# Macaron block with routed experts: FFN tiles in a deeper pipeline, three indirect DMAs under way, and a memset of a scratch between each and the next

## What is computed

```python
x = x + 0.5 * ffn(layernorm(x))
x = x + attn(layernorm(x))
x = x + 0.5 * ffn(layernorm(x))

def ffn(x):                       # xf: (8192, 128)
    top1 = argmax(xf @ gate_w.T + gate_b)
    for e in range(8):
        h = relu(xf @ w1[e].T + b1[e])
        y = h @ w2[e].T + b2[e]
        out = out + where(top1 == e, y, 0)
```

## Time and profile before

| | |
|---|---|
| Median of 3 runs | 652.54 us (649.6 to 659.46) |
| Profiled execution | 652.16 us, span 650.3 us |
| TensorE busy | 487.5 us |
| VectorE busy | 330.1 us |
| ScalarE busy | 263.2 us |
| GpSimd busy | 266.8 us, of which 264.3 us indirect DMAs |
| Mean granted TensorE clock | 0.874 |

### The profile page before, as it was taken

How to read it: one execution, slowest core, us unless ns; L and a number is a source line. 1 busy time by engine, 2 the same in 40 slices (tenths; PEclk the granted TensorE clock), 3 DMA queues, 4 the chain that set the end, 5 groups by cost and what they waited for, 6 DMA issues and landing times.

```text
span 650.3 us, 13261 instructions
## 1 busy us (share of the span) xinstructions
PE 487.5 (75%) x3914; PEld 434.7 (67%) x3914; DVE 330.1 (51%) x1229; ACT 263.2 (40%) x862; POOL 266.8 (41%) x288
## 2 busy tenths in 40 slices
PE   3983323989997999937788738487599798398986
PEld 2972313878886988926666526356499788388885
DVE  2553451545553655525799548464175554144442
ACT  1310001443443444526797547342245434144442
POOL 1156275555554444410000631615442555545543
PEclk9999997999997999965798658555699989789999
DMA  9923311556656655263000100331254564465640
GB/s 244 350 45 133 111 54 66 195 188 210 229 181 201 222 206 209 90 181 90 2 3 2 44 26 7 134 105 35 94 191 178 177 209 180 155 219 177 218 168 18
DMA packets 73189, 90.21 MB, mean 139 GB/s; under 512 B 11517, under 2 KB 49666, under 8 KB 72992
## 3 DMA queue, kind: packets, MB, share of 16 engines
q1 hardware_dynamic: 63760, 71.24, 32.8%
q0 software_dynamic: 8640, 17.52, 8.4%
q10 hardware_dynamic: 720, 0.60, 0.4%
HBM read 23.82 MB, written 19.62 MB: 67 GB/s over the span
## 4 chain that ended last, share of the span: by engine, by line
PE 54%; another core or an unknown queue 12%; DVE 10%; issue 9%; ACT 7%; DMA 4%; SPq 1%; POOL 0%; ACTq 0%; POOLq 0%; DVEq 0%
PE bank L1044 19%; PE classes L1057 16%; PE classes L1044 4%; ACT hT L483 3%; PE classes L1000 3%; PE bank L1032 2%; PE bank L990 2%; PE bank L1087 2%; DVE row_max L868 2%; DVE probs L870 2%; DMA x<-y_rows,tile_rows 2%; PE bank L1122 1%; PE classes L1108 1%; ACT k_by_head L522 1%
## 5 line engine op out<-in xcount | busy, mean ns | idle before, releaser
L439 POOL DMA_INDIRECT sorted_rows<-x_sb,rows x128 | 123.5, 965 | 221.8 <-DVE rows L701 166.8
L483 ACT ACTIVATE hT<-bank,stage_w 128x128 f32<-128x128 f32 x426 | 125.7, 366 | 195.3 <-PE bank L1044 156.1
L1044 PE MATMUL bank<-xT,stage_w 128*128 128x128 f32 x852 | 135.4, 298 | 36.6 <-ACT xT L475 28.9
L1057 PE MATMUL classes<-w_sb,hT 128*128 x1136 | 157.7, 284 | 0.1
L1044 PEld LDWEIGHTS bank<-xT,stage_w 128*128 128x128 f32 x852 | 112.6, 201 | 58.4 <-issue 58.2
L1057 PEld LDWEIGHTS classes<-w_sb,hT 128*128 128x128 f32 x1136 | 145.4, 200 | 0.6 <-issue 0.5
L447 POOL DMA_INDIRECT out_x<-y_rows,tile_rows x71 | 70.4, 991 | 78.6 <-DVE y_rows L799 42.0
L447 POOL DMA_INDIRECT x<-y_rows,tile_rows x71 | 70.4, 991 | 78.4 <-DMA x<-y_rows,tile_rows 28.2
L782 DVE TENSOR_SCALAR hT<-classes,stage_w 128x128 f32<-128x128 f32 x142 | 49.6, 349 | 101.6 <-PE classes L1044 64.0
L799 DVE SCALAR_TENSOR_TENSOR y_rows<-classes,residual 128x128 f32<-128x128 f32 x142 | 41.4, 291 | 73.2 <-PE classes L1057 49.0
L773 DVE TENSOR_SCALAR x_stage<-tile_rows 128x128 f32<-128x128 f32 x142 | 50.6, 358 | 23.2 <-DMA tile_rows<-sorted_rows 22.7
(11 more groups left out here) (114 smaller groups left out, 516.6 us busy)
## 6 DMA issues: line engine op xcount, KB each, us to landing
stage_w<-w_pack SPq DMA_DIRECT2D x142, 322.0 KB
tile_rows<-sorted_rows SPq DMA_DIRECT2D x142, 68.0 KB
x_sb<-x SPq DMA_DIRECT2D x16, 268.0 KB, 5.3
x_sb<-in_x SPq DMA_DIRECT2D x16, 256.0 KB, 5.5
w_pack<-in_w SPq DMA_DIRECT2D x1, 2048.0 KB, 9.5
w_sb<-in_w SPq DMA_DIRECT2D x1, 2048.0 KB, 10.6
sorted_rows<-x_sb,rows POOLq DMA_INDIRECT x128
sorted_rows<-filler SPq DMA_DIRECT2D x17, 68.0 KB
```

The costliest lines, as they stand in the source:

```text
L439: pool.indirect_dma_start(out=sorted_rows, out_offset=bass.IndirectOffsetOnAxis(ap=rows[k][:, t:t + 1], axis=0), in_=x_sb[:, groups[k][0] ...
L483: last = nc.scalar.activation(hT[:, n % 2, c, :], bank[n % 2][:, c * P:(c + 1) * P], ACT.Relu, bias=bias)
L1044: last = nc.tensor.matmul(mine, stage_w[:, w, c * P:(c + 1) * P], xT[:, n % 2, :], start=True, stop=True)
L1057: last = nc.tensor.matmul(bank[4 + n % 2][:, 0:D], hT[:, n % 2, c, :], w2_sb[:, bass.ds(expert, 1), c, :], start=(c == 0), stop=(c == HC - 1))
```

## The change

- Between two indirect DMAs GpSimd sets a scratch of 128x256 float32 to zero. A memset waits only for the memset before it.
- Three indirect DMAs are under way instead of two (`UNDER_WAY`).
- `pool_order`: the last group's 16 scatters are no longer paired with outputs. In the first FFN they come before all outputs, in the second after 14 outputs.
- SyncE: for the second and third span the rows of the first two quads are loaded before the weights of the first.
- The FFN tiles: four buffers for `x_stage` and `xT`, three for `hT`, `residual` and the hidden result's bank; TensorE's order becomes hidden(i), transpose(i + 2), output(i - 2). VectorE copies the transposed tile instead of ScalarE, ScalarE takes all four relus. VectorE normalizes four tiles ahead.
- `rank` of the last group comes after tile 12; ScalarE's and VectorE's waits for the expert weights before the first FFN are gone, as the weights' own slots are waited for.

```diff
+    AHEAD = 2
+    DEEP = 4
+    HIDDEN = 3
+    UNDER_WAY = 3
...
-        ahead = (0, 12)[f]
-        pool_order += early + outs[:ahead]
-        for row, tile in zip(final, outs[ahead:ahead + len(final)]):
-            pool_order += [row, tile]
-        pool_order += outs[ahead + len(final):]
+        ahead = (0, 14)[f]
+        pool_order += early + outs[:ahead] + final + outs[ahead:]
...
+    PAUSE = 256
...
-    RANK_TILE = 14
+    RANK_TILE = 12
...
                     sp.wait_ge(tabled, list_no[f, g] + 1)
-                    stage_weights(f, *quads[0])
+                    if g == 1:
+                        stage_weights(f, *quads[0])
                     wait_landed(sp, pool_no["rows", (f, g), groups[f, g][1] * R - 1])
...
-                        if q >= 2:
+                        if q >= 2 or g > 1:
                             stage_weights(f, *quads[q - 1])
...
             for q, item in enumerate(pool_order):
+                if q:
+                    if q >= 2:
+                        pool.wait_ge(paused, q - 1)
+                    nc.gpsimd.memset(pause[:], 0.0).then_inc(paused, 1)
...
-                    if q >= 2:
-                        pool.wait_ge(landed[q % 2], 16 * (q // 2))
+                    if q >= UNDER_WAY:
+                        pool.wait_ge(landed[q % UNDER_WAY], 16 * (q // UNDER_WAY))
...
-                    pool.wait_ge(y_ready, number(f, i) + 1)
-                    pool.wait_ge(landed[q % 2], 16 * (q // 2))
+                    pool.wait_ge(y_ready if f == 0 else y_summed, number(f, i) + 1)
+                    pool.wait_ge(landed[q % UNDER_WAY], 16 * (q // UNDER_WAY))
...
-                copy_xT(0)
                 for i in range(WORK):
                     relu(i)
-                    if i + 1 < WORK:
-                        copy_xT(i + 1)
...
-                stage(0)
-                stage(1)
-                for i in range(WORK):
-                    relu(i)
-                    if i + 2 < WORK:
-                        stage(i + 2)
-                    if i >= 1:
-                        take_output(i - 1)
-                    if i >= 2:
-                        dve.wait_ge(y_summed if f == 0 else y_ready, number(f, i - 1))
-                    add_residual(i)
-                    if f == 0 and i >= 1:
-                        take_moments(i - 1)
+                for i in range(DEEP):
+                    stage(i)
+                for i in range(AHEAD):
+                    copy_xT(i)
+                for i in range(WORK + AHEAD):
+                    if i + AHEAD < WORK:
+                        copy_xT(i + AHEAD)
+                    if i + DEEP < WORK:
+                        stage(i + DEEP)
+                    if i < WORK:
+                        add_residual(i)
+                    if i >= AHEAD:
+                        take_output(i - AHEAD)
+                    if f == 0 and i >= AHEAD + 1:
+                        take_moments(i - AHEAD - 1)
...
+                for i in range(AHEAD):
+                    transpose_x(i)
                 for i in range(WORK):
                     hidden(i)
-                    if i + 1 < WORK:
-                        transpose_x(i + 1)
-                    if i >= 1:
-                        output(i - 1, of_quad[(i - 1) % QUAD])
+                    if i + AHEAD < WORK:
+                        transpose_x(i + AHEAD)
+                    if i >= AHEAD:
+                        output(i - AHEAD)
```

More of the change, by code:

```diff
@@ L273, in macaron_kernel @@
         inv_sum = sb("inv_sum", [P, R * CLASS_HEADS])
+        pause = sb("pause", [P, PAUSE])
         attended = sb("attended", [P, 2, R * CLASS_HEADS, HEAD_DIM])
@@ L292, in macaron_kernel @@
         routed, tabled = sem("routed"), sem("tabled")
-        landed = [sem(f"landed{s}") for s in range(2)]
+        landed = [sem(f"landed{s}") for s in range(UNDER_WAY)]
         pads_stored = sem("pads_stored")
+        paused = sem("paused")
         rows_loaded = [sem(f"rows_loaded{q}") for q in range(QUADS)]
@@ L318, in ranks_of @@
             if k[1] == LAST:
-                return bank[7][:, 0:n]
+                return bank[3][:, 0:n]
             return bank[4][:, 256:256 + n]
         def wait_landed(eng, q):
-            for m in (q - 1, q):
-                if m >= 0:
-                    eng.wait_ge(landed[m % 2], 16 * (m // 2 + 1))
+            for m in range(max(q - UNDER_WAY + 1, 0), q + 1):
+                eng.wait_ge(landed[m % UNDER_WAY], 16 * (m // UNDER_WAY + 1))
         def load4(eng, which, table, i, top):
@@ L935, in _ @@
             whole(list_tiles((0, 3)))
-            dve.wait_ge(pack_loaded, 48)
             experts(0, {})
@@ L1039, in hidden @@
                     pe.wait_ge(xT_copied, n + 1)
+                    if n >= HIDDEN:
+                        pe.wait_ge(relu_done, n + 1 - HIDDEN)
                     for c in range(HC):
-                        mine = bank[n % 2][:, c * P:(c + 1) * P]
-                        if c >= HC_ACT:
-                            mine = bank[2 + n % 2][:, (c - HC_ACT) * P:(c - HC_ACT + 1) * P]
-                        last = nc.tensor.matmul(mine, stage_w[:, w, c * P:(c + 1) * P], xT[:, n % 2, :], start=True,
+                        last = nc.tensor.matmul(bank[n % HIDDEN][:, c * P:(c + 1) * P],
+                                                stage_w[:, w, c * P:(c + 1) * P], xT[:, n % DEEP, :], start=True,
@@ L1045, in hidden, with output @@
                                                 stop=True)
-                        if c == HC_ACT - 1:
-                            last.then_inc(h_a_done, 1)
-                    last.then_inc(h_v_done, 1)
-                def output(i, expert):
+                    last.then_inc(h_done, 1)
+                def output(i):
                     n = number(f, i)
                     if n >= 2:
-                        pe.wait_ge(y_ready, n - 1)
+                        pe.wait_ge(y_summed, n - 1)
+                    pe.wait_ge(relu_done, n + 1)
@@ L1054, in output @@
                     for c in range(HC):
-                        if c in (0, HC_ACT):
-                            pe.wait_ge(relu_a if c == 0 else relu_v, n + 1)
-                        last = nc.tensor.matmul(bank[4 + n % 2][:, 0:D], hT[:, n % 2, c, :],
-                                                w2_sb[:, bass.ds(expert, 1), c, :], start=(c == 0), stop=(c == HC - 1))
+                        last = nc.tensor.matmul(bank[4 + n % 2][:, 0:D], hT[:, n % HIDDEN, c, :],
+                                                w2_sb[:, bass.ds(expert[i], 1), c, :], start=(c == 0), stop=(c == HC - 1))
@@ L1059, in output, with load_experts @@
                     last.then_inc(y_done, 1)
                 listed = {spans[k][0]: list_no[k] for k in spans if k[0] == f}
-                transpose_x(0)
+                expert = {}
+                def load_experts(i):
+                    if i in listed:
+                        pe.wait_ge(tabled, listed[i] + 1)
+                    for j, value in enumerate(load4(pe, ENGINE.PE, expert_of[f], i, E - 1)):
+                        expert[i + j] = value
+                for i in range(AHEAD):
+                    transpose_x(i)
@@ L1073, in experts @@
                     if i in chores:
                         chores[i]()
-                output(WORK - 1, of_quad[(WORK - 1) % QUAD])
+                for i in range(WORK - AHEAD, WORK):
+                    output(i)
             def attention_step(j):
```

81 lines of the change are left out of this document (34 added, 47 removed).

## The result

| | before | after |
|---|---|---|
| Median | 655.12 us (649.6 to 659.46, 4 runs) | 613.27 us (609.37 to 617.15, 4 runs) |
| Profiled execution | 652.16 us, span 650.3 us | 617.15 us, span 615.3 us |
| End of first FFN, end of attention, span | 281.3, 451.2, 650.3 us | 269.9, 427.8, 615.3 us |

The ratio is 0.9388 with a 95% interval of 0.928 to 0.949: faster by 6.1%, a little under half of the 13% that was forecast. 613.27 us lies within the range of 540 to 643 us and far from 568 us.

A forecast was written before the change was run, and what follows sets the result against it. TensorE was taken as the bound at 2.14 us per FFN tile, plus late answers, border holes and small waits; gains of 31 (first FFN), 26 (attention) and 27 us (second FFN), 84 together, gave 568 us, range 540 to 643 us with rivals.

The forecast's parts named there:

- the pace that the memset gives: Indirect DMA streams on GpSimd: 0.96 + 0.30 + 0.30 us and a little issue time, 1.6 us per scatter; bounds 1.3 and 1.86 us.
- nearly all of the 61 us go: FFNs and attention: late TensorE answers under five scatter streams cost 61 us, and the memset removes nearly all of it.
- So 2.14 us stay: FFN tiles: TensorE's instructions are the same after the pipeline edits, so each tile still takes 2.14 us.
- small waits: Second FFN: twelve small TensorE waits of the two-deep pipeline, 8.0 us; the text says 5 of 8 go, the sum takes 8.
- First tile at 78 us: First FFN: without 16.2 us of late answers, the routing chain starts tiles at 78 us instead of 94.1 us.
- source 1: FFNs and attention: TensorE's answers come late while GpSimd streams indirect DMAs, 61 us in all, 16.2 us in 38 to 68 us.
- With the pause it is worth nothing more: GpSimd's streams: a third indirect DMA under way would shorten streams alone, but adds nothing once the memset is there.
- Holes at borders: Where a tile group begins, TensorE waits for rows (4.13, 3.23, 9.84 us); SyncE's new order leaves 1 or 2 us per border.
- Engines exchanged at no cost: FFN tiles: ScalarE and VectorE exchange a copy and a relu, both staying under 1.3 us where 2.14 are available.
- Rival 1: Scatter streams: the pause cures nothing and late answers have another cause, such as instruction loading; 630 to 655 us, chance 0.15.
- Rival 2: First FFN: without a cure, unbroken output streams hold up TensorE like scatters, 51 us more, about 693 us; chance 0.07.
- Rival 3: Both FFNs: at a pace of 1.86 us GpSimd becomes the bound, 621 us; chance 0.10 for 605 to 665 us.

## Why the forecast was wrong

**Failed step: the pace that the memset gives, and with it the cure.** The prediction added 0.30 us of memset to the 0.30 us that stood ahead of a scatter and "a little issue time", 1.6 us. The memset took 0.33 us and the gap ahead of the scatter shrank to 0.17 us: 1.46 us. The bounds of 1.3 to 1.86 us held it, but the faster end was used only as a gain (TensorE the bound, less 9 us in the range), while a faster pace brings the late answers back. On the changed kernel, with three under way:

| pace | VectorE's long waits for TensorE in the FFNs | time |
|---|---|---|
| 1.27 us | up to 18.2 us | 641.8 us |
| 1.46 us | 2.5 to 5 us, each tile | 613.3 us |
| 1.57 us | 2.3 to 3.1 us, six | 571.2 to 584.9 us |
| 1.63 us | 2.3 to 3.7 us, six | 572.0 us |
| 1.79 us | one of 2.45 us, GpSimd the bound | 602.7 us |
| 2.10 us | one of 2.42 us, GpSimd the bound | 685.2 us |

The sentence "nearly all of the 61 us go" rested on that 1.6 us, and on outputs at 1.75 us with landings between them, a broken stream. The other end of its comparison, "1.28 us without a break", was read wrongly too: the stream of the 12.36 us had a gap of 1.14 us in it.

At the pace it assumed, the time is 572 us against 568 us forecast, and by stages too the sum fits: the first FFN ends at 256.5 us (forecast 250), and attention and second FFN take 144 and 172 us, as forecast. Part of that is luck. The prediction gave the third indirect DMA under way nothing, and it is worth 7% there; it kept a tile at 2.14 us, and it fell to 1.90 us; and it had GpSimd catch up at the end of the second FFN, where at 1.63 us its last output starts 11.7 us behind VectorE's last result (567.26 and 555.58 us).

**"So 2.14 us stay".** Wrong, to the good: with TensorE busy without a break at full clock in both, a tile takes 2.14 us before and 1.90 us now, 17 us for 71 tiles. The eight matmuls of the hidden layer take 0.89 us of the chain instead of 0.91 + 0.22. The kernel before keeps its 2.14 us with either memset, with two and with three under way, and the changed kernel has its 1.90 us without the memset too, so the gain is of the FFN's edits; which of them brings it was not tried. Where GpSimd ends an FFN it doesn't show in the time.

**Where the 49.3 us are.** The span is 615.3 us, not 566. The first FFN ends 19.9 us late (TensorE stands still 21 us in 88 to 133 us), the attention lasts 157.9 instead of 144 us (13.2 us of late answers), and the second FFN 187.5 instead of 172 us (4.9 + 14.3 us lost in two stretches, a hole of 5.8 us). These are more than the second FFN's 15.5 us; that the cheaper tiles give the rest back is argued, not measured. In that FFN the sum also took all 8 us of small waits, where the text before it lets 5 of them go.

**First tile at 78 us.** Right: 78.38 us, against 94.18 us without the memset. Of source 1 the first 16 us did go.

**"With the pause it is worth nothing more" (three under way).** Wrong in both directions. At 1.63 us the third is worth 0.956 - 0.887 = 7% in the changed kernel and 5% in the kernel before, since a landing that takes longer than two paces no longer holds GpSimd. At 1.46 us it costs the kernel before 5%, as it makes the stream unbroken; in the changed kernel it changes little (0.946 to 0.939): late answers come, and the landings' holds go. That these two cancel is argued, not measured apart.

**Holes at borders.** Forecast 1 to 2 us each; 5.37 and 5.80 us came. With 128x448 and three under way the holes over 2.4 us add up to 3.64 + 6.61 + 4.44 = 14.7 us in the changed kernel and 2.79 + 4.68 + 2.90 + 8.42 = 18.8 us in the kernel before: SyncE's order, the order of the indirect DMAs and the deeper pipeline together mend 4 us of them. Which of them does was not tried apart. "Rows of tile 40 without a hole over 3 us" did not come true: the hole before that group is 5.80 us. All edits besides memset and third under way are worth 0.901 - 0.887 = 1.4%, 9 us (19 us by the medians, on two chips), where the prediction had 12 + 8 us for the holes and small waits of the second FFN alone.

**Engines exchanged at no cost.** Right: TensorE is busy 56.48 of 57 us in 133 to 190 us.

**Rival 1, the pause cures nothing.** Out: 0.989 without, 0.939 with it, 0.887 with a wider one. The instruction queue brought 35 packets, 34 before, and in the changed kernel 35 with the late answers and without them (128x448).

**Rival 2, outputs hold TensorE up as scatters do.** Its mechanism is real, at 1.28 us (17.19 us). It did not act here, because the outputs had the pause too.

**Rival 3, GpSimd the bound.** Its sum was good. For a pace of 1.79 us it gives 35.75 + 132 x 1.79 + 2.4 = 274.4 us for the end of the first FFN; 128x640 ended it at 274.6 us. It doesn't bind at 1.46 us. So the best pace stands between two walls 0.3 us apart (1.46 and 1.79 us), and the change was on the wrong side of the first.

## What to carry to other kernels

When a cure works by a spacing, measure the spacing that it really gives, and work out both sides of it: the price of too close is not the mirror of too far. A change that only removes waits (here the third under way) can lose more than it brings if those waits were breaking up a pattern that hurts another engine; try it with and without the cure. In the kernel before, the third under way turned 0.962 into 1.008 beside the narrow memset and 0.947 into 0.901 beside the wider one. A filler's width is one number: try three of it before anything of more work.

## What the hardware showed

TensorE's results reach VectorE and ScalarE late while GpSimd issues indirect DMAs close behind each other (in the changed kernel VectorE takes a result 5.4 us after its matmuls end). It depends on the gap between them: with three under way, gaps of 0.31 us give waits up to 18.2 us, of 0.50 us 2.5 to 5.8 us, of 0.66 us six of at most 3.7 us, with scatters and with outputs (17.19 us at a gap of 0.30 us), with a memset in the gap or with nothing. At 0.50 us it depends too on some gaps being longer. At a pace of 1.46 us the tiles lock to the stream, one in five scatters. By what path TensorE's answer is held, and what ends the hold, was not found.

VectorE's x_stage doesn't run beside GpSimd's memset. With a memset of 0.97 us it ends as the memset ends (GpSimd's row first, 100.27 + 0.97 = 101.24 us; VectorE's 99.87 + 1.45 = 101.32 us), and what stands behind it in VectorE's queue ends with it:

```profile
100.27 0.97 POOL L441 MEMSET pause<- 128x1024 f32 x1
```

```profile
99.87 1.45 DVE L772 TENSOR_SCALAR x_stage<-tile_rows 128x128 f32<-128x128 f32 x1
100.13 1.19 DVE L787 SCALAR_TENSOR_TENSOR residual<-stage_w,tile_rows 128x128 f32<-128x128 f32 x1
```

The mean of x_stage is 345 ns without a memset, 437 with 128x256, 508 with 128x448 and 1049 with 128x1024. The Trainium skill, SBUF — State Buffer, section "SBUF: two separate sides", has GpSimd and VectorE's two-port operations exclude each other at a shared pair of ports. These runs agree that one is held for the other's whole time. The page also has the one that starts first keep the ports; in the two rows shown VectorE's starts first by the profile, and is the one held. What it costs a tile is 0.09 us at 128x256, a third of the 0.30 us that the prediction drew from it. VectorE's spare time hides it, as said: TensorE is busy 56.48 of 57 us beside it.
